# A four-layer graph network on one core: fixed ranges of 128 nodes in place of 52 pieces of the edge list with moving windows

## The chip, the cores and the metric

The kernel runs on one core of a Trainium2 chip. Times are device microseconds (us) of one execution. The profile is one more execution, recorded by the hardware profiler; its length is called the span. Lower is better.

## The reference

There are 6,250 nodes with 128 features and 206,250 directed edges, sorted by their destination; 6,250 of them go from a node to itself. Each edge has a source, a destination and 128 attributes of its own. Four layers follow one another, each with a residual and a layer norm:

```python
# layer 0: sums of the edge attributes by destination
agg = segment_sum(edge_attr, receivers); h = relu([agg, x] @ W1 + b1) @ W2 + b2
# layer 1: attention of 8 heads of 16; the softmax runs over ALL edges of a head
score = clip(sum(Q[dst] * K[src]) / 4, -5, 5); out[dst] += softmax(score) * V[src]
# then @ WO, layer norm, two-layer MLP, layer norm
# layer 2: an MLP for each edge, summed by destination, then an MLP for each node
e = relu([x[src], x[dst]] @ We1 + be1) @ We2 + be2; agg[dst] += e
# layer 3: graph convolution with degrees
agg[row] += x[col] / sqrt(deg[row] * deg[col]); out = agg @ W.T + b
```

The receivers of layer 0 are the sorted destinations. All data are float32, the indices int32.

## The kernel before

**Tiling.** Features lie on the 128 partitions and nodes on the columns, in an array of 6,656 columns (52 blocks of 128). The edge list is cut into NG = 52 pieces ("groups") of 31 x 128 = 3,968 rows; the last piece overlaps the one before. The destinations of a piece lie in a window of 128 nodes that starts at the piece's first destination. Where it starts is computed on the chip (`base`), and each use of a window first loads the value of `base` into a register (`window_start`, L153). Should a window not hold all destinations of a piece, a second pass would follow; the number of passes and rounds is found on the chip too (`passes0`, `rounds`), and is one for these inputs.

**Stage `prepare` (L217).** SP loads the indices and the weights. VectorE takes the minimum and maximum of each piece's destinations from an array `dst_i` with the pieces on 13 partitions (L263, L264), converts the indices, and makes for all edges at once the place in the window (`rel`), the block of 128 nodes in which the source lies (`bucket`), and the source's place in it (L269 to L288, `targets_of_pass` L194). Two of these arrays are also stored to DRAM (`sort_rel`, `sort_ids`, L232 to L235) for later.

**Stage `edge_sums_and_lists` (L441), layer 0's edges.** A loop over the 52 groups. SP loads 3,968 rows of attributes (L450). VectorE and ScalarE build a one-hot matrix of the destinations for each chunk of 128 rows (L565 for 19 chunks; L490 and L494 for 12), and TensorE multiplies it with the attributes, 24 chunks first (L638) and the other 7 later (L643). The result is added to the window (L586). In the same loop the edges of a group are sorted by the block of their source, for all later layers: a one-hot of the block (`bucket_hot`, L366), counts of each chunk (totals, L372), prefix sums over chunks and rows (L379, L383), the rank of each edge in its block (L390, L404), a one-hot of the rank (L408), and a product that puts the packed number of each edge in its slot (`pay` on POOL L415, codes L396), which is turned (L660) and stored as the group's list (L515). A list has 50 tiles of 128 slots: 49 blocks of sources and one tile for edges of a node to itself.

**Order.** TensorE's order in the loop is written out by hand: turn, sum of 24 chunks, totals of the next group, sum of the other 7, prefix of the next group, codes of this one. VectorE's is `rank_step` (chosen, reduce, the next bucket_hot, rank one-hot), target one-hot, add. Buffers are double.

**Edge layers 1 to 3.** `layer1_edges` (L1149) runs over 26 pairs of groups and in each group over the 50 tiles, in 13 batches of four. For each tile it builds a one-hot from the list on VectorE and ScalarE, gathers the rows of the sources with it on TensorE (L1360), gathers the queries of the window (L1363), and sums the messages by destination (L1375). `layer2_edges` (L1618) does the same for layer 2 (L1840, L1843, L1854, L1856; VectorE L1679 to L1703). It also counts the degrees and the edges to itself in two rows `counts`. `layer3_edges` (L2086) takes the blocks of sources by fours ("quads", 13 of them), and for each quad goes round all groups: counts (L2171), evacuation on ScalarE (L2147), spread (L2179), and after each quad an add of 512 columns (L2121). It first loads the window of each group from DRAM (`load_windows`, 52 transfers on two queues, L2081). At the end of each of these stages one group is prepared again for a further round (`resort_*`, L879 to L976), from `sort_rel` and `sort_ids`.

**Node stages.** `layer0_nodes` (L1020) takes 13 steps of two lanes of 256 nodes; the others take wide steps of four lanes and a rest of two. POOL splits the rows into bfloat16 parts (L815 to L826) for the gathers, and they are stored to DRAM. `layer2_nodes` (L1913) first turns the two rows of counts into columns with 104 matmuls of one column (L1918).

The lines in which a group's pieces and its windows come from:

```python
def load(j, b, at):
    sp.wait_ge(summed0, j + 1)
    sp.dma_start(edges[b][:, :, :], edge_attr[at, :].rearrange("(p c) f -> p c f", c=G)).then_inc(edges_in[b], 16)
```

Of the kernel before, what the change touches and what calls it, by code (L numbers as in the profile page):

```python
# [5 lines left out]
P = 128  # L6
D = 128
HEADS = 8
HEAD = D // HEADS
HIDDEN = 512  # L10
G = 31
SC = G * P
W = P
U = 1
T = 256
TJ = T // P
LANES = 2
LN_EPS = 1e-5
CLIP = 5.0

# [15 lines left out]
def sizes(n_nodes, n_edges):  # L36

    node_cols = -(-(n_nodes + W) // (LANES * T)) * LANES * T
    groups = -(-(-(-n_edges // SC)) // 4) * 4
    return node_cols, groups, groups  # L40


def gnn_program(nc, xT, edge_attr, src_index, src_id, dst_id, dst_rows, consts,
                w1, w2, wqkv, wo, aw1, aw2, we1, we2, wn1, wn2, w3t, vectors, row_bqkv, row_be1, row_be2, out):
    NODES = xT.shape[1]
    NG = src_id.shape[1] // G
    E = edge_attr.shape[0]
    NTILES = NODES // T
    STEPS = NTILES // LANES
    HI = NODES // P  # L50
    NB = HI - 3
# [4 lines left out]
    PAIRS = NG // 2  # L56
    SPR = NG // 4
    PASSES_MAX = NODES // W + 1
    ROUNDS_MAX = SC // P + 1
    assert SPR <= P and E >= SC and HI <= P and NG >= 4 and NODES < 2 ** 15 and BUCKETS <= 50  # L60
    ctx = ExitStack()
    with ctx:
# [26 lines left out]
        band = sb("band", [P, 2 * G - 1], BF16)  # L89
        before = sb("before", [G, G], BF16)  # L90
# [21 lines left out]
        base0 = sb("base0", [1, NG])  # L112
        n_passes = sb("n_passes", [1, 2])
# [15 lines left out]
        y_rows = dram("y_rows", (NODES, 3 * D), BF16)  # L129
        lists = dram("lists", (NG, 2, TILES * P), I16)  # L130
        sort_rel = dram("sort_rel", (P, NG, G))
        sort_ids = dram("sort_ids", (P, NG, 2, G), BF16)

# [7 lines left out]
        def passes0(eng):  # L141

            return eng.value_load(loops[0:1, 0:1], min_val=PAIRS, max_val=PAIRS * PASSES_MAX)

        def rounds(eng):

            return eng.value_load(loops[0:1, 1:2], min_val=PAIRS, max_val=PAIRS * PASSES_MAX * ROUNDS_MAX)
# [5 lines left out]
        def window_start(eng_type, g):  # L153

            return nc.values_load_multi_w_load_instructions(base[0:1, ds(g, 1)], engines=(eng_type,),
                                                            min_val=0, max_val=NODES - W)[1][0]
# [11 lines left out]
        rows_loaded = sem("rows_loaded")  # L168
        const_set = sem("const_set")
        dst_minmax = sem("dst_minmax")  # L170
        low_ready = sem("low_ready")
        range_max = sem("range_max")
        passes_set = sem("passes_set")
        split_ids = sem("split_ids")
        wq_scaled = sem("wq_scaled")
        biases_spread = sem("biases_spread")
        sort_stored = sem("sort_stored")
        moved0 = sem("moved0")
        prep_dma = 15
        MOVE = 4  # L180

        sort_scope = ExitStack()
        rel = sb("rel", [P, NG, G], scope=sort_scope)
        bucket0 = sb("bucket0", [P, NG, G], BF16, scope=sort_scope)
        lo1 = sb("lo1", [P, NG, G], BF16, scope=sort_scope)
        bucket = sb("bucket", [P, NG, G], BF16, scope=sort_scope)
        dr1 = sb("dr1", [P, NG, G], BF16, scope=sort_scope)
        inside = sb("inside", [P, NG, G], scope=sort_scope)
        rank_by4 = sb("rank_by4", [P, P, 4], BF16, scope=sort_scope)

        def flat(t):
            return t[:, :, :].rearrange("p s g -> p (s g)")

        def targets_of_pass(dve, done, by):  # L194

            dve.tensor_scalar(flat(inside), flat(rel), float(P), None, ALU.is_lt).then_inc(moved0, by)
            dve.wait_ge(moved0, done + by)
            dve.scalar_tensor_tensor(flat(inside), flat(rel), 0.0, flat(inside), ALU.is_ge, ALU.mult).then_inc(moved0, by)
            dve.wait_ge(moved0, done + 2 * by)
            dve.scalar_tensor_tensor(flat(bucket), flat(bucket0), 1.0, flat(inside), ALU.add,  # L200
                                     ALU.mult).then_inc(moved0, by)
            dve.tensor_scalar(flat(dr1), flat(rel), 1.0, None, ALU.add).then_inc(moved0, by)
            dve.wait_ge(moved0, done + MOVE * by)

        with ExitStack() as prep_scope:
            dst_i = sb("dst_i", [P, 4, SC], I32, scope=prep_scope)
            src_e = sb("src_e", [P, NG * G], I32, scope=prep_scope)
            dst_e = sb("dst_e", [P, NG * G], I32, scope=prep_scope)
            parts_e = flat(inside).bitcast(I32)
            src_f = sb("src_f", [P, NG * G], scope=prep_scope)  # L210
            same_e = sb("same_e", [P, NG * G], BF16, scope=prep_scope)[:, :]
            low_sb = sb("low_sb", [P, 8], scope=prep_scope)
            small = sb("small", [1, 4], scope=prep_scope)
            small_i = sb("small_i", [1, 4], I32, scope=prep_scope)
            bqkv_sb = sb("bqkv_sb", [1, 3 * D], scope=prep_scope)
            be1_sb = sb("be1_sb", [1, 2 * D], scope=prep_scope)
            with nc.Block("prepare") as block:  # L217
                @block.sync
                def _(sp):
                    sp.dma_start(dst_i[0:SPR, :, :], dst_rows).then_inc(rows_loaded, 16)  # L220
                    sp.dma_start(cst[:, :], consts).then_inc(rows_loaded, 16)
                    sp.dma_start(dst_e[:, :], dst_id).then_inc(rows_loaded, 16)
                    sp.dma_start(src_e[:, :], src_id).then_inc(rows_loaded, 16)
                    for tile, src in ((x, xT), (wqkv_sb, wqkv), (wo_sb, wo), (aw1_sb, aw1),
                                      (aw2_sb, aw2), (we2_sb, we2), (wn2_sb, wn2), (w3t_sb, w3t), (vec, vectors),
                                      (bqkv_sb, row_bqkv), (be1_sb, row_be1), (be2_sb, row_be2)):
                        sp.dma_start(tile[:, :], src).then_inc(loaded, 16)
                    sp.dma_start(we1_sb[:, 0:D], we1[0:D, :]).then_inc(loaded, 16)
                    sp.dma_start(we1_sb[:, D:2 * D], we1[D:2 * D, :]).then_inc(loaded, 16)
                    sp.dma_start(wn1_sb[:, :, :], wn1.rearrange("(b p) n -> p b n", p=P)).then_inc(loaded, 16)  # L230
                    sp.wait_ge(range_max, 4)
                    sp.dma_start(sort_rel, rel[:, :, :]).then_inc(sort_stored, 16)  # L232
                    sp.wait_ge(split_ids, 7)
                    sp.dma_start(sort_ids[:, :, 0, :], bucket0[:, :, :]).then_inc(sort_stored, 16)
                    sp.dma_start(sort_ids[:, :, 1, :], lo1[:, :, :]).then_inc(sort_stored, 16)  # L235
                    sp.wait_ge(sort_stored, 48)
                    sp.wait_ge(loaded, 16 * prep_dma)

                @block.vector
                def _(dve):  # L240
                    dve.memset(ones[:, :], 1.0).then_inc(const_set, 1)
# [170 lines left out]
        def pay_with(eng, pay, hot, vals):  # L412

            for w in range(2):
                last = eng.tensor_tensor(pay[:, :, w, :], hot[:, 0:G, :], over_columns(vals[w], BUCKETS), ALU.mult)  # L415
# [1969 lines left out]
```

## Time and profile before

| | before |
|---|---|
| median of 3 runs | 5670.74 us (5668.15 to 5678.23) |
| profiled execution | 5659.9 us span; a time of its own outside the span is not listed, the median of the runs is 10.8 us above it |
| TensorE busy | 5214.6 us (92%), 58,522 matmuls |
| VectorE busy | 4413.4 us (78%) |
| ScalarE busy | 3424.0 us (60%) |
| POOL busy | 2023.7 us (36%) |
| moved by DMA | 523.77 MB, mean 93 GB/s |

PE is TensorE's matmul, PEld its weight load, DVE VectorE, ACT ScalarE, SP the engine that issues most transfers. "SPq" and "ACTq" mark the issue of a transfer by that engine's queue. Busy time excludes waiting. The span falls into the start (to 117 us), layer 0's edges (to 777), its nodes (796 to 1019), layer 1's edges (1048 to 3053) and nodes (3086 to 3295), layer 2's edges (3327 to 4706) and nodes (4767 to 4886), layer 3's edges (4935 to 5533) and nodes (5565 to 5660).

### The profile page before, as it was taken

How to read it: one execution, taken by the hardware profiler on the slowest of the kernel's cores; microseconds unless marked ns; L12 is line 12 of the kernel's file. 1: busy time of each engine (PE TensorE's matmuls, PEld its weight loads, DVE VectorE, ACT ScalarE, POOL GpSimd, SP SyncE). 2: the span in 40 equal slices, each digit the busy share in tenths (PEclk: the TensorE clock that was granted, in tenths of full speed). 3: DMA queues.
4: the chain of work that ended last, by engine and by line, in shares of the span. 5: the costliest groups of instructions: out<-in, count | busy, mean ns of one | idle time of the engine just before them, and what ended most of it. 6: DMA issues, size and time to landing. Idle time of an engine off the chain costs nothing. (4 is left out here: it accounts for less than half of the span.)

```text
span 5659.9 us, 172717 instructions
## 1 busy us (share of the span) xinstructions
PE 5214.6 (92%) x58522; PEld 4657.6 (82%) x58522; DVE 4413.4 (78%) x7814; ACT 3424.0 (60%) x6098; POOL 2023.7 (36%) x1980
## 2 busy tenths in 40 slices
PE   2999989799999999999997879999999997699996
PEld 1888877699999999999997769999999996466655
DVE  6888852577777777777776669999999994488886
ACT  1445534577777777777774447777777772366651
POOL 1444436333333333333332545555555552300000
PEclk9999999899999999999998989999999997899998
DMA  6444421222222222222221133333333330200000
GB/s 108 158 164 169 162 81 67 95 96 93 89 95 95 87 95 95 89 94 95 91 91 39 50 104 129 134 130 134 131 134 128 136 129 19 67 1 0 0 0 25
DMA packets 206220, 523.77 MB, mean 93 GB/s; under 512 B 33555, under 2 KB 85398, under 8 KB 199318
## 3 DMA queue, kind: packets, MB, share of 16 engines
q1 hardware_dynamic: 195936, 518.35, 27.1%
q10 hardware_dynamic: 10179, 4.02, 0.3%
q8 instruction: 65, 1.06, 0.1%
q14 instruction: 40, 0.33, 0.0%
HBM read 485.12 MB, written 37.19 MB: 92 GB/s over the span
## 5 line engine op out<-in xcount | busy, mean ns | idle before, releaser
L1360 PE MATMUL ps<-kv_table,stage 128*128 128x256 bf16 x7644 | 1252.2, 273 | 29.9 <-ACT stage L1273 29.8
L1650 POOL TENSOR_TENSOR parts<-rest 128x512 bf16<-128x512 f32 x624 | 699.5, 1130 | 618.6 <-DVE rest L1703 618.5
L1840 PE MATMUL ps<-a_table,stage 128*128 128x128 bf16 x7644 | 842.6, 219 | 32.4 <-DVE stage L1679 32.4
L1843 PE MATMUL ps<-window,stage 128*128 128x128 bf16 x7800 | 861.1, 219 | 0.0
L1363 PE MATMUL ps<-window,stage 128*128 128x128 bf16 x7800 | 860.2, 219 | 0.0
L1331 POOL TENSOR_TENSOR message<-message 128x512 f32<-128x512 f32 (+1 forms) x468 | 472.7, 1010 | 948.8 <-ACT message L1280 948.8
L1196 DVE TENSOR_TENSOR product<-ps,q_kept 128x512 f32<-128x512 f32 (+1 forms) x676 | 452.3, 669 | 394.6 <-ACT message L1259 319.8
L1257 ACT ACTIVATE q_kept<-ps 128x512 f32<-128x512 f32 (+1 forms) x676 | 392.2, 580 | 576.9 <-PE ps L1363 568.0
L1360 PEld LDWEIGHTS ps<-kv_table,stage 128*128 128x128 bf16 x7644 | 669.4, 98 | 71.4 <-issue 30.4
L1363 PEld LDWEIGHTS ps<-window,stage 128*128 128x128 bf16 x7800 | 654.5, 98 | 59.3
L1759 ACT ACTIVATE parts<-ps 128x512 bf16<-128x512 f32 x624 | 370.2, 593 | 326.1 <-PE ps L1843 326.0
L1840 PEld LDWEIGHTS ps<-a_table,stage 128*128 128x128 bf16 x7644 | 534.7, 98 | 32.9 <-issue 32.9
L2179 PE MATMUL ps<-pairs,y_window 128*128 128x512 bf16 (+1 forms) x2028 | 532.8, 372 | 27.7 <-ACT pairs L2147 27.6
L1843 PEld LDWEIGHTS ps<-window,stage 128*128 128x128 bf16 x7800 | 545.5, 98 | 0.0
L2147 ACT ACTIVATE pairs<-ps 128x512 bf16<-128x512 f32 (+1 forms) x676 | 386.6, 572 | 260.1 <-PE ps L2171 211.4
L1375 PE MATMUL ps<-message,slot_hot 128*128 128x136 f32 x3536 | 514.3, 287 | 26.0 <-POOL message L1331 25.9
L1854 PE MATMUL ps<-parts,slot_hot 128*128 128x258 bf16 x2496 | 490.2, 273 | 2.1 <-DVE slot_hot L1695 1.6
L1856 PE MATMUL ps<-rest,slot_hot 128*128 128x128 bf16 x2600 | 475.9, 221 | 0.0
L1375 PEld LDWEIGHTS ps<-message,slot_hot 128*128 128x128 f32 x3536 | 442.1, 190 | 39.9 <-POOL message L1331 21.8
L1200 DVE TENSOR_REDUCE score<-product 128x32 f32<-128x512 f32 (+1 forms) x676 | 449.9, 666 | 23.9 <-DVE product L1196 0.9
L415 POOL TENSOR_TENSOR pay<-bucket_hot,vals 128x1550 bf16<-128x1550 bf16 x104 | 286.6, 2777 | 477.5 <-DVE rank_hot L408 368.8
L1208 DVE TENSOR_TENSOR slot_hot<-iota,slots 128x512 f32<-128x512 f32 (+1 forms) x676 | 452.9, 670 | 0.0
(359 smaller groups left out, 11002.7 us busy)
## 6 DMA issues: line engine op xcount, KB each, us to landing
stage<-lists SPq DMA_DIRECT2D x312, 768.0 KB, 4.1
edges<-in_edge_attr SPq DMA_DIRECT2D x52, 1984.0 KB, 7.6
stage<-lists SPq DMA_DIRECT2D x104, 896.0 KB, 5.4
window<-qkv_rows SPq DMA_DIRECT2D x52, 288.0 KB, 4.6
qkv_rows<-kv_table SPq DMA_DIRECT2D x26, 384.0 KB, 2.5
window<-ab_rows SPq DMA_DIRECT2D x52, 192.0 KB, 4.4
qkv_rows<-q_parts SPq DMA_DIRECT2D x26, 192.0 KB, 2.0
ab_rows<-a_table SPq DMA_DIRECT2D x26, 192.0 KB, 2.0
```

Of the source, the lines that this page charges most:

```text
L1196: dve.tensor_tensor(product[:, 0:nt, :], kv_ps[n % 2][:, 0:nt, 0:D], q_kept[n % 2][:, 0:nt, :], ALU.mult).then_inc(product1, 1)
L1208: dve.tensor_tensor(slot_hot[n % 2][:, 0:nt, :], over_chunks(iota1[:, :], nt), over_columns(slots[:, ds(g, 1), 0, 4 * b:4 * b + nt] .rearr ...
L1331: pool.tensor_tensor(values, values, message[n % 3][:, 0:nt, D:D + HEADS].unsqueeze(3) .broadcast_to([P, nt, HEADS, HEAD]), ALU.mult).then ...
L1360: nc.tensor.matmul(kv_ps[n % 2][:, i, :], from_src, kv_table[:, tile, q, :], start=(q == 0), stop=(q == 2))
L1363: last = nc.tensor.matmul(q_ps[n % 2][:, i, :], own, window[d][:, q * D:(q + 1) * D], start=(q == 0), stop=(q == 2))
L1375: last = nc.tensor.matmul(ps[:, 6 + d, 0:D + HEADS], slot_hot[n % 2][:, i, :], message[n % 3][:, i, :], start=(tile == 0), stop=(tile == S ...
L1650: pool.tensor_tensor(parts_of(n)[:, 0:nt, D:2 * D], rest[BUFFER[n]][:, 0:nt, :], middle[BUFFER[n]][:, 0:nt, :], ALU.subtract).then_inc(low ...
L1840: nc.tensor.matmul(to[:, i, :], from_src, a_table[:, tile, q, :], start=(q == 0), stop=False)
L1843: last = nc.tensor.matmul(to[:, i, :], own, window[d][:, (3 + q) * D:(4 + q) * D], start=False, stop=(q == 2))
L1854: nc.tensor.matmul(ps[:, 6 + d, 0:DIRECT], slot_hot[BUFFER[n]][:, :, i], parts_of(n)[:, i, :], start=(tile == 0), stop=False)
L1856: last = nc.tensor.matmul(ps[:, 6 + d, DIRECT:SUMS], slot_hot[BUFFER[n]][:, :, i], middle[BUFFER[n]][:, i, :], start=False, stop=(tile == ...
L2179: last = nc.tensor.matmul(ps[:, 4 + quad % 2, 0:nt * P], y_window[:, ds(i * 4 + d, 1), q * D:(q + 1) * D] .rearrange("p s f -> p (s f)"), ...
```

## The change

Groups are no longer pieces of equal length. There are NG = 49 fixed ranges of 128 nodes; group g has the nodes from 128 g on, and its part of the edge list is a piece of up to 35 chunks (SG = 4,480 rows) whose first row is found on the chip.

- The node arrays have 6,272 columns for 6,656. Windows need no `base`.
- In the start, the numbers of all edges (destination's block, place in the block, source's place, source's block; four bfloat16, 8 bytes a row) are computed in SBUF and stored to DRAM as `ids_rows`. The largest block in each run of 58 rows gives, by a comparison with all 49 groups and two reductions, the run in which each group begins (`best`, `low`, `begins`), and from it `base` (the piece's first row, at most E - SG) and `skip`. The minimum and maximum over `dst_i` go, and so do the stores `sort_rel` and `sort_ids`. `prepare` and `rounds` are no blocks of their own any more. Memsets of acc, slots, z_sum and deg are on POOL, the loads of x and of the sources on ScalarE's queue.
- In layer 0's loop, SP loads each group's numbers (4,480 rows of 8 bytes, 280 bytes a partition) two groups ahead. VectorE picks the rows that belong to the group (`id_step`, at the start of `rank_step`) before it builds bucket_hot; ScalarE's targets wait for it. ScalarE's copies `vals` (L484, L485) are gone, POOL reads the numbers. VectorE builds 20 chunks of targets, TensorE's first block has 27.
- The list's tile of edges of a node to itself takes those of the nodes whose place in their block is under 120.
- Node stages take 7 steps of 896 nodes (lanes of 256, 256, 256 and 128). Layer 0's are done by two lanes at a time, of 512 and 384 nodes.
- Edge layers run over 24 pairs and one single group. Layer 2's add has one more instruction for the edges to itself (`self_dis`), counts is one row, and `group_sum` has two buffers (TensorE's group matmuls wait for added2). The 104 matmuls of L1918 go.
- Layer 2's node steps put the parts of y in SBUF for layer 3 (`y_window`); the store `y_rows` and `load_windows` go.
- The group that is prepared again is loaded by one transfer of its numbers, and picked with 3 instructions for 5.

Counted from the reference's inputs, the largest range has 4,401 edges, or 4,408 with the rounding to runs of 58 rows; the largest list tile has 126 of 128 slots (124 for the edges to itself). So there is one pass and one round.

```diff
-G = 31
+G = 406
 SC = G * P
+RUN = 58
+RUNS = G // RUN
+GC = 35
+SG = GC * P
...
-    node_cols = -(-(n_nodes + W) // (LANES * T)) * LANES * T
-    groups = -(-(-(-n_edges // SC)) // 4) * 4
+    node_cols = -(-n_nodes // P) * P
+    chunks = -(-(-(-n_edges // SC)) // 4) * 4
...
+            def begins(dve, done, by):
+
+                dve.tensor_scalar(wanted[:, :], low[:, :], current[:, 0:1], None, ALU.add).then_inc(begun, by)
+                dve.wait_ge(begun, done + by)
+                dve.tensor_scalar(begin[:, :], wanted[:, :], float(E - SG), None, ALU.min).then_inc(begun, by)
+                dve.wait_ge(begun, done + 2 * by)
+                dve.tensor_copy(base[:, :], begin[0:1, :])
+                dve.tensor_tensor(skip[:, :], wanted[:, :], begin[:, :], ALU.subtract).then_inc(begun, by)
...
+                    sp.wait_ge(ids_stored, 48)
+
+                    sp.wait_ge(begun, 3)
+                    sp.wait_ge(passes_set, 1)
...
+                        def load_ids(g, b):
+                            at = first_edge(mybir.EngineType.SP, g)
+                            sp.dma_start(ids[:, ds(g, 1), :, :].rearrange("p s c w -> p (s c w)"),
+                                         ids_rows[ds(at, SG), :].rearrange("(p c) w -> p (c w)", c=GC)
+                                         ).then_inc(ids_in[b], 16)
+
+                        def load_edges(j, g, b):
+                            at = first_edge(mybir.EngineType.SP, g)
                             sp.wait_ge(summed0, j + 1)
                             sp.sem_inc(sp_waited, 1)
-                            sp.dma_start(edges[b][:, :, :], edge_attr[at, :].rearrange("(p c) f -> p c f", c=G)
+                            sp.dma_start(edges[b][:, :, :], edge_attr[ds(at, SG), :].rearrange("(p c) f -> p c f", c=GC)
                                          ).then_inc(edges_in[b], 16)
...
+                    dve.tensor_reduce(top[:, :], blocks_of(0, CH), AX.X, ALU.max).then_inc(edge_blocks, 1)
+                    dve.wait_ge(edge_blocks, 1)
+                    dve.wait_ge(const_set, 18 + CH)
+                    dve.tensor_tensor(reach, over_columns(iota[:, 0:NG], SUBS), over_chunks(top[:, :], NG), ALU.is_le
+                                      ).then_inc(edge_blocks, 1)
+                    dve.wait_ge(edge_blocks, 2)
+                    dve.tensor_tensor(keyed, reach, over_chunks(key_low[:, :], NG), ALU.mult).then_inc(edge_blocks, 1)
+                    dve.wait_ge(edge_blocks, 3)
+                    dve.tensor_reduce(best[0][:, :], keyed, AX.X, ALU.max).then_inc(edge_blocks, 1)
...
+                    def id_step(j, g, b, load):
+                        numbers = ids[:, ds(g, 1), :, :].rearrange("p s c w -> p (s c) w")
+                        dve.wait_ge(ids_in[b], load * 16 + 16)
+                        dve.wait_ge(hot_act0, j + 1)
+                        dve.tensor_scalar(owned[:, :], place[:, :], skip[:, ds(g, 1)], None, ALU.is_ge).then_inc(selected, 1)
+                        dve.wait_ge(selected, j * 2 + 1)
+                        inside_dve(dve, inside[:, :], owned[:, :], numbers[:, :, 0], g).then_inc(selected, 1)
+                        dve.wait_ge(selected, j * 2 + 2)
+                        dve.tensor_tensor(bucket[b][:, :], numbers[:, :, 3], inside[:, :], ALU.mult)
+                        dve.tensor_tensor(target[b][:, :], numbers[:, :, 1], inside[:, :], ALU.mult).then_inc(split_ids, 1)
...
+        LANES = ((0, T), (T, T), (2 * T, T), (3 * T, P))
...
-                        dve.tensor_tensor(counts[:, ds(at, P)], counts[:, ds(at, P)], GROUP_COUNTS, ALU.add)
...
+                        dve.tensor_tensor(self_dis[:, ds(g, 1)], self_dis[:, ds(g, 1)],
...
+        y_window = sb("y_window", [P, NG, 3, D], BF16)
...
-                    for c in range(HI):
-                        last = nc.tensor.matmul(ps[:, 7, c:c + 1], counts[:, c * P:(c + 1) * P], self_row[:, :],
-                                                start=True, stop=True)
...
-            def load_windows(eng, eng_type, odd):
```

## Rows read from the trace of the kernel before

**Rows 1.** Busy time by stretch: stretch, length, busy us (instructions) of each engine, granted clock, DMA.

```profile
core 0: us, PE busy (x) PEld busy (x) DVE busy (x) ACT busy (x) POOL busy (x), PEclk, DMA share, GB/s
...
777.00:796.00 19.00, 2.50 (x26) 1.67 (x23) 10.27 (x23) 2.31 (x5) 0.00 (x0) 0.64 0.14 44
796.00:1019.00 223.00, 216.64 (x988) 175.13 (x988) 56.16 (x130) 100.38 (x232) 134.29 (x194) 0.99 0.18 64
...
1048.00:3053.00 2005.00, 1963.39 (x20904) 1843.83 (x20904) 1563.48 (x3015) 1415.51 (x2495) 692.83 (x676) 1.00 0.26 92
...
3086.00:3295.00 209.00, 176.49 (x1040) 153.27 (x1040) 130.39 (x363) 90.90 (x297) 104.10 (x194) 0.96 0.14 45
...
3327.00:4706.00 1379.00, 1375.51 (x21216) 1355.60 (x21216) 1342.32 (x2079) 1007.69 (x1142) 732.21 (x676) 1.00 0.37 130
...
4767.00:4886.00 119.00, 116.10 (x572) 86.37 (x572) 50.27 (x152) 54.11 (x162) 51.25 (x97) 0.95 0.12 38
```

**Rows 2.** Timeline of one group of layer 0's loop: start us, us, engine, line, out<-in.

```profile
400.49 5.60 PE L638 MATMUL ps<-dst_hot,edges 128*128 128x128 f32 x48
...
406.02 0.97 PE L372 MATMUL ps<-bucket_hot,band 128*31 128x50 bf16 x31
...
406.92 1.83 PE L643 MATMUL ps<-dst_hot,edges 128*128 128x128 f32 x14
...
408.58 0.33 PE L379 MATMUL ps<-bucket_hot,lower 128*128 128x400 bf16 x1
...
408.88 0.29 DVE L586 TENSOR_TENSOR acc<-acc,ps 128x128 f32 x1 [0.27 <-PE ps L643]
...
410.82 1.60 PE L396 MATMUL ps<-pay,rank_hot 128*128 128x100 bf16 x31
...
413.12 5.60 PE L638 MATMUL ps<-dst_hot,edges 128*128 128x128 f32 x48
```

**Rows 3.** VectorE's groups in that loop: xcount | busy us, mean ns | idle before.

```profile
L565 DVE TENSOR_TENSOR dst_hot<-ps,rel 128x2432 f32<-128x2432 f32 x52 | 139.5, 2682 | 0.0
L408 DVE TENSOR_TENSOR rank_hot<-rank_by,rank_all 128x4096 bf16<-128x4096 bf16 x52 | 118.6, 2281 | 0.0
...
L390 DVE TENSOR_TENSOR chosen<-ps,bucket_hot 128x1600 f32<-128x1600 f32 x52 | 94.8, 1824 | 97.1 <-PE ps L383 97.1
L404 DVE TENSOR_REDUCE rank_all<-chosen 128x1600 f32 (+1 forms) x52 | 94.6, 1820 | 7.8 <-DVE chosen L390 7.8
```

**Rows 4.** Timeline of the start, 0 to 118 us.

```profile
2.38 5.61 DVE L245 MEMSET acc<- 128x6656 f32 x1 [1.38 <-issue]
...
16.56 0.15 DVE L253 TENSOR_SCALAR lane<-cst 128x1 f32<-128x1 f32 x1 [5.47 <-DMA src_e<-in_src_id]
...
34.36 16.66 DVE L264 TENSOR_REDUCE low_sb<-dst_i 13x4 f32<-13x15872 int32 x1
...
56.75 1.84 DVE L276 SCALAR_TENSOR_TENSOR lo<-bucket,src_f 128x1612 bf16<-128x1612 bf16 x1
...
107.09 1.77 DVE L366 TENSOR_TENSOR bucket_hot<-ps,bucket 128x1550 bf16<-128x1550 f32 x1 [0.38 <-DVE list_b L554]
...
117.28 6.96 PE L638 MATMUL ps<-dst_hot,edges 128*128 128x128 f32 x48
```

**Rows 5.** Timeline of the start of layer 3's edges.

```profile
4903.47 1.29 PE L2171 MATMUL ps<-src_hot,dst_hot 128*128 128x128 bf16 x8 [18.13 <-DVE src_hot L2113]
...
4934.00 1.57 ACT L2147 ACTIVATE pairs<-ps 128x512 bf16<-128x512 f32 x3 [48.71 <-issue]
```

**Rows 6.** The add after each quad of layer 3: duration min/median/max, first and last start.

```profile
L2121 DVE TENSOR_TENSOR acc<-acc,ps x11: 686/686/689, 5029.1 to 5489.3; 128x512 f32<-128x512 f32 x11
```

**Rows 7.** DMA issues: count, KB each, median us from issue to landing.

```profile
sort_rel<-rel SPq DMA_DIRECT2D x1, 806.0 KB, 3.7
...
sort_ids<-lo SPq DMA_DIRECT2D x1, 403.0 KB, 35.6
...
stage<-sort_ids SPq DMA_DIRECT2D x2, 15.5 KB, 1.7
```

**Rows 8.** Timeline ahead of layer 2's node steps.

```profile
4741.29 22.34 PE L1918 MATMUL ps<-self_row,counts 2*128 2x1 f32 x104 [3.47 <-DVE self_row L1977]
```

More of the change, by code:

```diff
@@ new lines, in node_tiles, with norm_pe @@
+            tiles["inv"] = [sb(f"inv{layer}_{l}", [P, T // P], scope=scope) for l in range(lanes)]
+            return tiles
+        ALL = range(ROUND)
+        def norm_pe(pe, t, nth, ready, before_ready, lanes=ALL, bank=half, buffer=lambda l: l):
+            for k, l in enumerate(lanes):
+                b = buffer(l)
+                pe.wait_ge(ready, before_ready + k + 1)
+                nc.tensor.matmul(bank(b, 1)[:, 0:width(l)], centre_m, t["res"][b][:, 0:width(l)], start=True, stop=True
+                                 ).then_inc(centred_ps, 1)
+            for k, l in enumerate(lanes):
+                b = buffer(l)
+                pe.wait_ge(squared, nth + k + 1)
+                for j in range(blocks(l)):
+                    last = nc.tensor.matmul(bank(b, 2)[:, j:j + 1], t["sqr"][b][:, j * P:(j + 1) * P], mean_col[:, :],
@@ L1488, in _ @@
+                        norm_act(act, t, nth1(n, 2))
+                        for l in ALL:
+                            act.wait_ge(normed, nth1(n, 2) + l + 1)
+                            act.activation(x[:, columns(n, l)], t["y"][l][:, 0:width(l)], ACT.Copy).then_inc(x_kept, 1)
+                    with loop(act, 0, STEPS) as n:
+                        step(n)
                 @block.vector
@@ L1566, in _ @@
+                    with loop(sp, 0, STEPS) as n:
+                        step(n)
+                    for l in ALL:
+                        sp.wait_ge(ab_stored[l], STEPS * 32 + 32)
                         sp.sem_inc(sp_waited, 1)
@@ new lines, in add, with body @@
+                        dve.tensor_tensor(counts[:, ds(g * P, P)], counts[:, ds(g * P, P)], GROUP_COUNTS, ALU.add)
+                        dve.tensor_tensor(acc[:, ds(g * P, P)], acc[:, ds(g * P, P)], GROUP_ACC, ALU.add).then_inc(added2, 1)
+                    def body(j, g, behind, groups=2):
+                        for n in range(groups * BATCHES):
+                            d, b = n // BATCHES, n % BATCHES
+                            if n + 1 < groups * BATCHES:
+                                rest_of(j + (n + 1) // BATCHES, n + 1)
+                            elif groups == 2:
+                                rest_of(j + 2, 0)
+                            slots_of(j + d, g + d, n)
@@ L1966, in step @@
+                        for l in ALL:
                             act.wait_ge(normed, nth2 + first + l + 1)
[L1967 to L1969 removed]
+                            act.activation(x[:, columns(n, l)], t["y"][l][:, 0:width(l)], ACT.Copy).then_inc(x_kept, 1)
+                    with loop(act, 0, STEPS) as n:
+                        step(n)
                 @block.vector
@@ L2222, in _ @@
+                            four(first, quad, 0, begin=True)
+                            with loop(pe, 1, FOURS - 1) as i:
+                                four(first, quad, i)
                             four(first, quad, FOURS - 1, end=True)
+                            if quad + 1 < QUADS:
+                                count(first, quad + 1, 1, 1)
+                            spread(first, quad, NG - 1, 0, end=True)
                         resort_pe(pe, again, step3, first, again_total)
```

2143 lines of the change are left out of this document (1113 added, 1030 removed).

## The prediction

> **What bounds the kernel now.** I read the busy times by stretch first, since the mean share of TensorE over the span says nothing of one stage. In the three long edge stretches TensorE is busy for 1963 of 2005 us, 1375.5 of 1379 us and, in the node steps between, 217 of 223 us, at a granted clock of 0.99 to 1.00, which is the upper level, 2.4 GHz [rows 1]. VectorE follows it closely only in layer 2 (1342 of 1379). So what counts is how many matmuls the program has, and the edge stages have a fixed number for each group. Then I read one group of the first loop in order of time [rows 2] and VectorE's groups of the same loop [rows 3]; there the reader is to see that TensorE goes from one matmul block to the next without a gap, and that VectorE's only long idle time is the wait for the prefix sums (97 us in 52 groups). Last come the stretches in which TensorE has nothing to do: the first 117 us, the seams between layers and the 29 us ahead of layer 3's first spread [rows 4, 5].
>
> **The edge layers, groups of a fixed cost.** A group keeps 50 tiles of 128 slots whatever its number of edges; 49 groups for 52 take three away. Layer 1: 2005 / 52 = 38.56 us each [rows 1], times 3 is -116. With 24 pairs and one single group the last one has no partner to overlap; I bound that at 16 us (under half a group): -116 to -100. Layer 2: 1379 / 52 = 26.52, times 3 is -80. It gains a VectorE instruction of 128x1 for each group; the nearest row is a 128x1 at 0.15 us [rows 4], 49 of them 7 us on an engine with 37 us to spare in that stretch: nothing, and +15 if its hand-off shows. The sums' second buffer makes TensorE wait for added2 where ScalarE waited before; queued behind that wait are the next tile's matmuls, but the add that it waits for is a group (26 us) old. Layer 3: one quad goes round all groups in 46.02 us, (5489.3 - 5029.1) / 10 [rows 6]; 46.02 x 3 / 52 = 2.65 less, for 12 full quads and a shorter 13th at about 2.5: -34.
>
> **Layer 0's loop, fewer groups of more chunks.** Here the edges are the same, and a piece grows from 31 to 35 chunks, so this goes up. The period now is 413.12 - 400.49 = 12.63 us [rows 2]: sums 5.53 + 1.66, totals 0.90, prefix 2.24, codes 1.60 and 0.70 up to the next sum. Chunks scale by 35/31, the prefix by 9/8 (nine chunks to a bank for eight): 8.12 + 1.02 + 2.52 + 1.81 + 0.70 = 14.17. Times 49 is 694, against 12.63 x 52 = 657: +38. VectorE's work for a group by the same scaling [rows 3]: chosen 2.05, reduce 2.05, buckets 1.99, ranks 2.57 (36 columns of chunks for 32), targets 2.82 (20 chunks for 19), add 0.29 [rows 2], and four id instructions of 35 columns, by the 128x1 at 0.15 about 0.75 with two hand-offs: 12.5 us. (Buckets from the 1.77 in [rows 4].) It stays 1.6 under TensorE's 14.17. The id step stands between the reduce and the bucket instruction, and delays the latter; from the prefix's end that is 2.05 + 2.05 + 0.75 + 1.99 = 6.8 us, and the totals that need it come 1.81 + 0.70 + 6.3 = 8.8 us after it. 2 us are over, so the added wait is hidden. ScalarE's target instructions now wait for the same step (split_ids); they start some 3 us later and have the whole sum block as cover. Bounds: +30 if the sums are a little better packed, +103 if VectorE becomes the bound at 15.5 us a group.
>
> **The ids' loads.** Each group gets a 35 KB load from DRAM in 280-byte pieces, two groups ahead of its use, on SP's queue between the loads of the edges. The nearest row is a 15.5 KB load of the same fields at 1.7 us [rows 7]. Twice that is 3.5 us in a period of 14.17: cost nothing in the loop, 3.5 once at the start. SP's edge loads are queued behind the wait for the ids before; as these landed a group earlier, nothing waits. A row that bears against it is the removed store: 62-byte pieces took 35.6 us for 403 KB, long pieces 3.7 us for 806 KB [rows 7]. The Trainium skill ("DMA: Bandwidth & Descriptors", Specifications) says that a transfer under 512 bytes loses the full rate because the DMA engine then reads, modifies and writes. By that page the loads would be slow and the sum 2 to 5 us higher at the start, no more while two groups of cover stand. The 15.5 KB load in 62-byte pieces, at 1.7 us, shows no such loss on the reading side, and the sum goes by it.
>
> **The start.** The first sum now begins at 117.28 [rows 4]. Two reductions over all targets on 13 partitions (16.7 us each, one behind the other) go, and so does the slow store with the barrier behind it: the last long field instruction of before starts at 56.75, the loop's first at 107.09. In their place the ids arrive at about 10 (four loads had landed by 16.56, and now the targets come first, the sources on ScalarE's queue); 8 field instructions at 1.84 are 14.7; 8 searches over 49 x 28 runs at about 1.5 (by size from the 1.84) are 12; some 25 small dependent instructions at 0.3 are 7.5; constants and conversions 5; together the first rows are known near 50. The long-piece store runs beside the searches. One id load and the loop's own 10.2 us from the bucket instruction to the first sum, 12 with 35 chunks, lead to 66: -51. Bounds: -62 if searches and fields overlap, -35 if each hand-off takes double. What is queued behind SP's new waits there (ids stored, first rows found, constants moved) is the first edge load, needed at about 66: on the path only if those waits end much after 55. The memsets of acc (5.61 us on VectorE [rows 4]) go to POOL, which has nothing else until 50: nothing lost, at most 6 us either way; with the x load moved to the other queue I put -2.
>
> **Seams and node steps.** The seam after layer 0's loop is 19 us, 10.3 of them VectorE's [rows 1]: the targets of a second pass are no longer made, and the limits come without a barrier of their own: -5 (-9 to 0). Layer 0's nodes: 13 steps took 223 us for 6656 columns; 6272 are 0.942 of that, -13 by columns, one step more gives back 2: -11 (+17 if POOL's splitting, 134 us busy, ends up behind the narrower steps). Layer 1's nodes: 209 us, -12 by columns, +11 for one more wide step and POOL's last splits: -1 (-12 to +8). Layer 2's, 119 us, -7 and +2: -5. Layer 3's, which move as many columns in as many steps, I scale from layer 2's: -4. The three places that redo a group for the lists now load the ids by one DMA and do 3 instructions for 5, but first wait for a value read on SP: +2 each, +6 (0 to +10).
>
> **Layer 2 to 3.** 104 matmuls of one column at the low clock, 22.34 us with all else waiting [rows 8], go with counts' second row: -23 with their hand-off. Layer 3 loaded its windows from DRAM in 52 transfers: the count ends at 4904.8 and the first evacuation starts at 4934.00 [rows 5]. Filled in SBUF by the node steps, it is there at once, and what is late next is the count itself: -29 (-20 if POOL's last splits are late).
>
> **Sum.** -116 - 80 - 34 + 38 - 51 - 2 - 5 - 11 - 1 - 5 - 4 + 6 - 23 - 29 = -317 us. The profiled span is 5659.9, so the span after is 5343; the median of the three times is 10.8 above the span, which gives **5354 us**.
>
> **Rivals.**
> A, layer 0's loop bound by VectorE. For it: 12.5 of 14.17 leaves little, and in [rows 3] its ends are dependent. Against: the 97 us of idle that are there now. At 15.5 us a group, 65 more: 5419.
> B, the id step exposed in each group: load landing and step stand ahead of the totals, 3.5 us x 49 = 172: 5526. Against: two groups of cover.
> C, slower: a group's rows don't fit its piece. The piece has 4480 rows and its start is only found to 58 rows; from 4480 on a second pass is made, of the loop (694) and, as each pass and round repeats it, of the edge stages (1889 + 1300 + 564) and of the redoing of 49 groups at each: some 17,700 us. By counting the inputs the largest range has 4401 edges, and 4408 with the rounding, so it should not come; only a mistake of the search on the chip would bring it.
> D, the fixed ranges bring nothing: the edge stages are bound by tiles in use, not by groups. Against it stand 52 equal group times; then the 230 us of the edge layers stay, and only the other terms hold: 5584.
>
> **How the numbers follow.** Forecast 0.82, A 0.09, B 0.03, D 0.02, C 0.03, and 0.01 for gains that meet losses within 0.2%, 11 us, which is about what a measurement of this kernel can tell. The forecast's own bounds added in part (start +16, single group +16, nodes +25; start -11, loop -8, seam and nodes -6) give 5329 to 5411; with A the range is 5315 to 5425, a little wider at both ends for what no row shows. Faster: 0.96, same 0.01, slower 0.03.
>
> **What would show it.** The first sum near 66 us. 14.2 us from sum to sum in layer 0, VectorE still idle ahead of chosen (about 1.5 us a group; none under A). Layer 1's edge stretch near 1889, layer 2's near 1300, quads at 43.4. No one-column matmuls ahead of layer 2's node steps, and the first evacuation of layer 3 within 2 us of the count. It would be wrong by A if the loop is 15.5, by a start later than 85, or by a node stage longer than before.

## The result, and the profile after

The changed kernel takes 5488.94 us (median of 4 runs, 5486.88 to 5493.09) against 5671.44 us for the kernel before (4 runs, 5668.15 to 5678.23): a ratio of 0.9678, interval 0.9665 to 0.9692. It is faster by 182 us where 317 were forecast, and lies outside the range of 5315 to 5425. The profiled span is 5485.0 us, 174.9 less than before. It lies 3.9 us under the median of the runs, where the forecast added 10.8: the forecast misses the span by 142 us and the time by 135, and these 7 us are luck.

Busy time by stretch of the changed kernel (columns as in [rows 1]):

```profile
0.00:70.00 70.00, 11.12 (x87) 6.67 (x87) 50.27 (x69) 18.70 (x28) 16.47 (x16) 1.00 0.44 167
70.00:824.00 754.00, 662.89 (x8664) 589.75 (x8662) 728.39 (x479) 350.46 (x956) 297.59 (x96) 1.00 0.40 148
...
838.00:1086.00 248.00, 209.50 (x1023) 168.87 (x1024) 60.22 (x135) 96.93 (x247) 141.76 (x224) 0.93 0.19 66
1086.00:2977.00 1891.00, 1850.12 (x19696) 1737.05 (x19696) 1471.60 (x2839) 1334.11 (x2350) 653.12 (x637) 1.00 0.26 92
2977.00:3263.00 286.00, 189.51 (x1142) 165.01 (x1143) 158.09 (x433) 97.43 (x329) 111.02 (x224) 0.82 0.13 40
3263.00:4586.00 1323.00, 1304.23 (x19983) 1278.92 (x19982) 1294.69 (x2004) 949.00 (x1076) 684.66 (x637) 1.00 0.36 128
4586.00:4767.00 181.00, 129.32 (x699) 98.40 (x699) 79.10 (x201) 54.21 (x179) 54.06 (x112) 0.77 0.00 1
4770.00:5356.00 586.00, 569.14 (x4224) 344.94 (x4297) 477.91 (x1277) 363.19 (x635) 0.00 (x0) 0.96 0.00 0
5356.00:5485.00 129.00, 85.41 (x615) 70.59 (x614) 79.26 (x250) 21.71 (x94) 0.00 (x0) 0.87 0.08 26
```

The second line is the one to stop at: in layer 0's loop VectorE is busy for 728 of 754 us and TensorE only for 663. Before, TensorE set the pace there. Against the forecast, by the marks in both traces (first sum, first gather, last group matmul of a layer, first count):

| stretch | before | after | difference | forecast |
|---|---|---|---|---|
| to the first sum | 117.3 | 70.0 | -47 | -53 |
| layer 0's loop and the seam | 678.5 | 767.8 | +89 | +33 |
| layer 0's nodes, to layer 1's first gather | 252.7 | 248.2 | -4.5 | -11 |
| layer 1's edges | 2005 | 1891 | -114 | -116 |
| one group again, layer 1's nodes | 274 | 285.5 | +11 | +1 |
| layer 2's edges | 1378.4 | 1324.5 | -54 | -80 |
| one group again, layer 2's nodes, to the first count | 198 | 180 | -18 | -26 |
| first count to first spread | 31.2 | 2.2 | -29 | -29 |
| layer 3's quads | 598.4 | 586.7 | -12 | -34 |
| one group again, layer 3's nodes | 126.9 | 128.6 | +2 | -2 |

Of the 142 us by which the span misses the forecast, the loop has 56, layer 2's edges 26, the quads 22, the start 6, and the node stages with what lies around them some 30.

One group of layer 0's loop after the change (answers to [rows 2]; start us, us, engine, line):

```profile
406.28 6.22 POOL L278 TENSOR_TENSOR pay<-bucket_hot,ids 128x1750 bf16<-128x1750 bf16 x2 [9.43 <-DVE rank_hot L271]
...
408.69 0.77 DVE L661 TENSOR_SCALAR owned<-place,skip 128x35 bf16<-128x35 f32 x1
408.75 1.65 PEld L260 LDWEIGHTS ps<-pay,rank_hot 128*128 128x128 bf16 x35
...
409.64 2.91 DVE L283 SCALAR_TENSOR_TENSOR inside<-ids,cst,owned 128x35 bf16<-128x35 bf16 x1 [0.19 <-DVE owned L661]
...
412.69 0.20 DVE L665 TENSOR_TENSOR bucket<-ids,inside 128x35 bf16<-128x35 bf16 x1
...
412.94 2.03 DVE L254 TENSOR_TENSOR chosen<-ps,bucket_hot 128x1800 f32<-128x1800 f32 x1
...
419.07 1.07 PE L236 MATMUL ps<-bucket_hot,band 128*35 128x50 bf16 x35 [1.52 <-DVE bucket_hot L230]
...
424.39 1.78 PE L260 MATMUL ps<-pay,rank_hot 128*128 128x100 bf16 x35
```

The period is 424.39 - 408.75 = 15.64 us here; over all groups it is 15.45 on average. POOL's pay is two instructions, 6.22 us in all, so the first ends near 409.4 and the second at 412.50. VectorE's owned, of 35 columns, ends at 409.46, and inside, of 35 columns too, at 412.55: each ends just after one of POOL's ends. That is no chance of this group: in each of the 48 groups whose step stands in the loop, inside ends between 0.05 and 0.06 us behind pay. And chosen, which could start once the prefix is done at 408.8, starts at 412.94; TensorE then waits 1.52 us for bucket_hot, ahead of the totals. The same two instructions while POOL is idle, in the start of the same trace:

```profile
33.51 0.40 SPq L372 DMA_DIRECT2D ids_rows<-dst_hot  x1
...
56.74 1.56 SPq L392 DMA_DIRECT2D ids<-ids_rows  x2
58.69 0.24 DVE L661 TENSOR_SCALAR owned<-place,skip 128x35 bf16<-128x35 f32 x1 [3.90 <-DMA ids<-ids_rows]
58.97 0.26 DVE L283 SCALAR_TENSOR_TENSOR inside<-ids,cst,owned 128x35 bf16<-128x35 bf16 x1
...
70.03 1.22 PE L798 MATMUL ps<-dst_hot,edges 128*128 128x128 f32 x4
```

0.24 and 0.26 us, against 0.77 and 2.91; POOL starts its first pay only at 62.04. The add (acc<-acc,ps) starts beside pay in each group too and keeps its 0.28 us; it reads one of its two operands from PSUM. Layer 2's added instruction shows the same pattern (timeline, then the same line's durations, min/median/max):

```profile
4003.69 1.05 POOL L1864 TENSOR_TENSOR parts<-rest 128x512 bf16<-128x512 f32 x1 [1.26 <-DVE rest L1923]
4003.77 0.99 DVE L1929 TENSOR_TENSOR self_dis<-self_dis,group_sum 128x1 f32 x1
...
L1929 DVE TENSOR_TENSOR self_dis<-self_dis,group_sum x49: 158/992/996, 3306.8 to 4587.4; 128x1 f32 x46, 128x1 f32<-128x1 f32 x3
```

It starts 0.08 us behind POOL's instruction and ends 0.02 us behind its end.

### The profile page after: what moved, and what is told of

Its sections match the earlier page's. It is cut to its first block and busy times, and to the rows that moved or that the text cites. A ratio compares the mean times of both kernels' runs of the same rounds, so it can differ in the third digit from the quotient of the medians.

```text
span 5485.0 us, 164969 instructions
## 1 busy us (share of the span) xinstructions
PE 5016.6 (91%) x56178; PEld 4464.3 (81%) x56254; DVE 4408.0 (80%) x7721; ACT 3289.6 (60%) x5897; POOL 1958.7 (36%) x1946
## 5 line engine op out<-in xcount | busy, mean ns | idle before, releaser
L1555 PE MATMUL ps<-kv_table,stage 128*128 128x256 bf16 x7203 | 1180.0, 273 | 29.7 <-ACT stage L1461 29.5
L1864 POOL TENSOR_TENSOR parts<-rest 128x512 bf16<-128x512 f32 x588 | 654.0, 1118 | 613.3 <-DVE rest L1923 607.0
L2062 PE MATMUL ps<-a_table,stage 128*128 128x128 bf16 x7203 | 794.6, 219 | 41.2 <-DVE stage L1899 41.2
L2065 PE MATMUL ps<-window,stage 128*128 128x128 bf16 x7350 | 812.1, 219 | 0.0
L1558 PE MATMUL ps<-window,stage 128*128 128x128 bf16 x7350 | 810.8, 219 | 0.0
L1555 PEld LDWEIGHTS ps<-kv_table,stage 128*128 128x128 bf16 x7203 | 629.5, 98 | 69.2 <-issue 30.3
L1558 PEld LDWEIGHTS ps<-window,stage 128*128 128x128 bf16 x7350 | 616.9, 98 | 55.9
L2062 PEld LDWEIGHTS ps<-a_table,stage 128*128 128x128 bf16 x7203 | 504.2, 98 | 41.8 <-issue 41.6
L2065 PEld LDWEIGHTS ps<-window,stage 128*128 128x128 bf16 x7350 | 514.5, 98 | 0.0
L1570 PE MATMUL ps<-message,slot_hot 128*128 128x136 f32 x3332 | 484.7, 287 | 24.3 <-POOL message L1519 24.3
L2372 PE MATMUL ps<-pairs,y_window 128*128 128x512 bf16 (+1 forms) x1835 | 490.9, 372 | 3.7 <-ACT pairs L2341 0.2
L278 POOL TENSOR_TENSOR pay<-bucket_hot,ids 128x1750 bf16<-128x1750 bf16 x98 | 303.8, 3121 | 502.7 <-DVE rank_hot L271 451.5
```

Source lines behind the costliest of these rows:

```text
L1555: nc.tensor.matmul(kv_ps[n % 2][:, i, :], from_src, kv_table[:, tile, q, :], start=(q == 0), stop=(q == 2))
L1558: last = nc.tensor.matmul(q_ps[n % 2][:, i, :], own, window[d][:, q * D:(q + 1) * D], start=(q == 0), stop=(q == 2))
L1570: last = nc.tensor.matmul(ps[:, 6 + d, 0:D + HEADS], slot_hot[n % 2][:, i, :], message[n % 3][:, i, :], start=(tile == 0), stop=(tile == S ...
L1864: pool.tensor_tensor(parts_of(n)[:, 0:nt, D:2 * D], rest[BUFFER[n]][:, 0:nt, :], middle[BUFFER[n]][:, 0:nt, :], ALU.subtract).then_inc(low ...
L2062: nc.tensor.matmul(to[:, i, :], from_src, a_table[:, tile, q, :], start=(q == 0), stop=False)
L2065: last = nc.tensor.matmul(to[:, i, :], own, window[d][:, (3 + q) * D:(4 + q) * D], start=False, stop=(q == 2))
```

## The experiments

Theory 1: a VectorE instruction with two operands in SBUF, or one with a single operand in a fast form, is held until POOL's running instruction ends; the step that the change adds was put where POOL is busy, in layer 0 and in layer 2. The rivals: VectorE simply has too much work (2), the ids arrive late (3), anything on VectorE beside pay is slow (4), layer 2 loses to its other new wait or to the single last group (5). The gains below compare medians with the changed kernel's 5488.94 us. The kernel before, measured along with each series, gave 5671, 5668 and 5666 us, so such a difference is good to some 5 us; the profiled spans fall by 52 us in e1, 73 in e2, 17 in e3 and 22 in e4.

**e1, the id step behind the reduce.**

```diff
-                        if load is not None:
-                            id_step(j + 1, g + 1, 1 - b, load)
                         dve.wait_ge(prefixed, j + 2)
...
                         if load is not None:
+                            id_step(j + 1, g + 1, 1 - b, load)
                             bucket_step(j + 1, 1 - b)
```

> The four id instructions stand behind the rank reduce in place of ahead of chosen; nothing else moves. Theory 1 (a VectorE instruction that reads two SBUF operands, or a single one in its fast form, is held until POOL's running pay instruction ends): at the new place pay is over, so the inside instruction takes about 0.26 us for 2.90, a group's period falls from 15.64 to 14.2 to 14.5 us, and the kernel from 5489 to about 5425 us. Rival 2 (VectorE has too much work in a group, wherever the step stands): inside stays near 2.9 us and the period at 15.6. Rival 3 (the ids' loads arrive late): the period stays and the wait for the load shows ahead of owned.

5432.67 us, ratio to before 0.9585 (0.9569 to 0.9601): 56 us off the changed kernel. VectorE's groups in the loop (answers to [rows 3]):

```profile
L254 DVE TENSOR_TENSOR chosen<-ps,bucket_hot 128x1800 f32<-128x1800 f32 x47 | 95.5, 2033 | 82.0 <-PE ps L247 82.0
...
L283 DVE SCALAR_TENSOR_TENSOR inside<-ids,cst,owned 128x35 bf16<-128x35 bf16 x46 | 11.8, 257 | 8.6 <-DVE owned L661 8.6
L661 DVE TENSOR_SCALAR owned<-place,skip 128x35 bf16<-128x35 f32 x46 | 10.8, 235 | 0.0
```

The same instructions are short at the other place, and the idle time ahead of chosen is back (82 us). Rival 2 falls. So does rival 3: there is no wait for a load ahead of owned here, and in the changed kernel only one, for the first group. From the codes of the first group to those of the last the period is 14.33 us.

**e2, the id step at its early place, its results in PSUM.**

```diff
-            owned = sb("owned", [P, GC], BF16, scope=scope)
-            inside = sb("inside", [P, GC], BF16, scope=scope)
+            owned = ps[:, 2, 256:256 + GC]
+            inside = ps[:, 2, 320:320 + GC]
...
```

> The id step stays at its early place, while pay runs, but owned and inside are written to PSUM, so that inside, bucket and target read one operand from SBUF and one from PSUM. Theory 1 in its narrow form (what is held is the second SBUF read): inside takes under 0.4 us with pay running, the period falls to 14.3 to 14.7 us, the kernel to about 5430 us. Rival 4 (any VectorE instruction of this kind that runs beside pay is slow): inside stays near 2.9 us and nothing changes. The owned instruction has one SBUF operand and a PSUM output now; if only it stays at 0.7 us, that was its wait for the first half of pay.

5415.29 us, ratio 0.9558 (0.9542 to 0.9573): 74 us off, 17 more than e1. Timeline of one group:

```profile
400.94 6.21 POOL L278 TENSOR_TENSOR pay<-bucket_hot,ids 128x1750 bf16<-128x1750 bf16 x2 [7.94 <-DVE rank_hot L271]
...
404.00 0.26 DVE L661 TENSOR_SCALAR ps<-place,skip 128x35 f32<-128x35 f32 x1
404.45 0.26 DVE L283 SCALAR_TENSOR_TENSOR ps<-ids,cst,ps 128x35 f32<-128x35 f32 x1 [0.19 <-DVE ps L661]
404.85 0.19 DVE L665 TENSOR_TENSOR bucket<-ids,ps 128x35 bf16<-128x35 f32 x1
...
405.98 2.03 DVE L254 TENSOR_TENSOR chosen<-ps,bucket_hot 128x1800 f32<-128x1800 f32 x1 [0.81 <-PE ps L247]
```

POOL's pay runs from 400.94 to 407.15, all three stand inside it, and none is held. So it is not POOL's running as such (rival 4 falls), but where the operands lie. Bucket and target still write to SBUF, have one operand in PSUM now, and take 0.19 us each beside pay: a write to SBUF alone is not held. Owned has the same inputs as before and only its output has moved; whether it was held for a fast form or for something else about that output no run tells apart. Chosen waits for TensorE again, and the period is 14.0 us, (754.8 - 82.8) / 48 from the first group's codes to the last's: a little under the 14.17 of the sum. The Trainium skill ("SBUF — State Buffer", Who interferes with whom) has the rule: VectorE and GpSimd (POOL) share one pair of SBUF ports as an exclusive lock, and whichever comes first keeps it for its whole instruction. A VectorE instruction with two SBUF inputs contends with a GpSimd instruction that reads SBUF, one in a 2-port mode with any; one with at most one SBUF input and outside these modes does not contend. The trace agrees: inside takes 2.91 us with both inputs in SBUF and 0.26 us with one in PSUM.

**e3, layer 2's add reads PSUM.**

```diff
                         dve.tensor_tensor(self_dis[:, ds(g, 1)], self_dis[:, ds(g, 1)],
-                                          group_sum[d][:, 2 * D + 1:DIRECT], ALU.add)
+                                          ps[:, 6 + d, 2 * D + 1:DIRECT], ALU.add)
...
                         if b == 0:
                             pe.wait_ge(group_sb2, j + 1)
+                            pe.wait_ge(added2, j + ready - 1)
```

> Layer 2 only: the added 128x1 instruction reads the group's sum from PSUM in place of SBUF, and TensorE's first scatter of a group waits for the add of two groups before. Theory 1: self_dis falls from 0.98 us to under 0.3, some 34 us of VectorE's time; the edge stretch of layer 2 goes from 1323 to about 1300 us, the kernel by as much. Rival 5 (the 26 us of layer 2 come from TensorE's wait for added2 or from the single last group): self_dis gets short, the stretch stays at 1323.

5468.2 us, ratio 0.9646 (0.963 to 0.9663): 21 us off. The line's durations:

```profile
L1929 DVE TENSOR_TENSOR self_dis<-self_dis,ps x49: 139/142/157, 3305.7 to 4567.7; 128x1 f32 x46, 128x1 f32<-128x1 f32 x3
```

0.142 us for 0.992, and layer 2's edges take 1306 us for 1324.5. Here only an input has moved to PSUM, and the output stays in SBUF. The kernel has one wait more on TensorE and is still faster, so rival 5 falls for 18 of the 26 us; the last few (1306 against some 1299 forecast) stay open.

**e4, layer 3 in turns of eight groups.** The quads took 45.1 us where 46.02 x 49 / 52 = 43.4 was forecast. Theory 6: the difference is what TensorE pays for each turn of its inner loop. Rival 7: it is the phase between the engines at the border of a quad.

```diff
-                            with loop(pe, 1, FOURS - 1) as i:
+                            with loop(pe, 1, FOURS - 1, 2) as i:
                                 four(first, quad, i)
+                                four(first, quad, i + 1)
```

> Layer 3 only: TensorE's inner loop takes eight groups a turn for four. Theory 6 (the 1.7 us that a quad takes over 49 x 0.882 us are TensorE's turns of the loop, some 0.13 us each with no instruction ready): half the turns, quads at about 44.4 for 45.1 us, some 8 us less in all. Rival 7 (it is the phase between the engines at the border of a quad): quads stay at 45.1 us.

5465.92 us, ratio 0.9644 (0.9627 to 0.966): 23 us off, three times what was expected. The adds after each quad (answer to [rows 6]), first of the changed kernel, then of e4:

```profile
L2315 DVE TENSOR_TENSOR acc<-acc,ps x13: 286/687/689, 4814.8 to 5356.1; 128x512 f32<-128x512 f32 x12, 128x128 f32<-128x128 f32 x1
```

```profile
L2315 DVE TENSOR_TENSOR acc<-acc,ps x13: 289/687/689, 4814.8 to 5333.9; 128x512 f32<-128x512 f32 x12, 128x128 f32<-128x128 f32 x1
```

Divided by 12 these are 45.1 and 43.3 us a quad. What the turn costs can be seen at TensorE's weight loads once in four groups, in the changed kernel:

```profile
5012.44 0.27 PEld L2364 LDWEIGHTS ps<-src_hot,dst_hot 128*128 128x128 bf16 x4 [0.43 <-issue]
...
5016.22 0.26 PEld L2364 LDWEIGHTS ps<-src_hot,dst_hot 128*128 128x128 bf16 x4 [0.49 <-issue]
```

and in the kernel before, in turns of four as well:

```profile
5131.96 0.27 PEld L2171 LDWEIGHTS ps<-src_hot,dst_hot 128*128 128x128 bf16 x4 [0.30 <-issue]
...
5135.45 0.32 PEld L2171 LDWEIGHTS ps<-src_hot,dst_hot 128*128 128x128 bf16 x4 [0.25 <-issue]
```

Before, the gap stays within the lead that weight loads have over the matmuls: around these two places the counts start evenly, 0.88 or 0.89 us apart. After, it is 0.13 to 0.24 us longer and the next matmul starts late, 1.01 and 1.07 us behind the count before it. In e4's trace, with eight groups a turn, the counts from 4945 to 4961 us are even again, through two turns. Rival 7 falls, and theory 6 holds in that longer turns take the loss away; my size, half of the loss, was too small. It is not the turn alone, since the kernel before had turns of four without a loss.

**e6, the same turns of four, code moved.** Theory 8: it matters where the loop's code lies.

```diff
+                    for _ in range(32):
+                        pe.sem_inc(pe_waited, 1)
                     with pe.Fori(0, total, NG) as first:
```

> Layer 3's turns of four groups as in the changed kernel, but with 32 more one-word instructions on TensorE's queue ahead of the loop, which shift where its code lies and cost about 1 us themselves. Theory 8 (what makes the turn cost is where the loop's code falls): the layer's stretch changes clearly, by 5 us or more from 586. Theory 6 in its plain form (a turn of four groups costs this wherever it lies): within 2 us of 586.

The adds of the quads:

```profile
L2315 DVE TENSOR_TENSOR acc<-acc,ps x13: 289/687/689, 4819.1 to 5360.2; 128x512 f32<-128x512 f32 x12, 128x128 f32<-128x128 f32 x1
```

(5360.2 - 4819.1) / 12 = 45.1 us, unchanged (5490.94 us, one run). This one shift of the code does not move it; other shifts were not tried. Why the turn is longer after the change than before, with the same number of matmuls in it, stays open.

**e5, all three.** The edits of e2, e3 and e4 together.

> The id step's two results in PSUM, layer 2's add from PSUM, and layer 3's turns of eight groups, together. The three places lie in stages that follow one another, so the gains should add: 74 + 21 + 23 = 118 us off 5489, which is 5371 us, 17 above the blind forecast. If one gain had only moved a wait that another stage gives back, the sum comes out smaller: over 5380 us.

5380.16 us (5375.16 to 5384.15), ratio to before 0.9497 (0.9484 to 0.951), the fastest of all. The median lies 9 us over the 5371 expected, just at the 5380 above which the expectation said that the gains do not add. But the 118 us were a sum of differences of medians from different series. By stage they add: the span is 5373.3, 112 less than the changed kernel's, and 73 + 17 + 22 = 112 are the three spans' gains one by one. The loop with its seam gives 70 of them, layer 2 takes 1303 us for 1324.5, and a quad 43.3. The time is 26 us over the blind forecast and the span 30, as much as the node stages and what lies around them missed, which none of the three edits touches.

## Why the prediction was wrong

**The mechanism was right for the groups.** Layer 1's three groups were worth 114 us for 116. The wait for windows went as forecast (-29), the stretch around the one-column matmuls gave 18 of 26, and the start brought 47 of 53. There the first rows were known at 43.4 us, before the 50 forecast, but the number of passes only at 54, a last link that my chain of searches did not have.

**The step that failed** is "four id instructions of 35 columns, by the 128x1 at 0.15 about 0.75 with two hand-offs: 12.5 us", then "It stays 1.6 under TensorE's 14.17", and with it "the added wait is hidden". By size the price was nearly right: they are 0.9 us of work in e1 and e2, 1.2 with the hand-offs. But I placed the step between the reduce and the bucket instruction; the code has it at the start of `rank_step`, ahead of chosen, as my own list of the changes says. There POOL's pay is running, and chosen started 412.94 - 408.69 = 4.25 us after the step did. With it VectorE's round is 15.5 to 15.6 us in most groups, not 12.5, and it sets the pace. I took the price of a small instruction from a row in which POOL is idle (0.15 us [rows 4]) and used it for a place where POOL is at work. Rival A had the right outcome for the loop (15.5 us a group, +65; measured 15.45 on average, and 56 over the forecast with the seam) with a chance of 0.09, but not the cause: it rested on 12.5 of 14.17 leaving little, and by work alone there was room enough (e2). Even where I had placed the step it would not have been hidden: e1 has it there and takes 14.42 us in most groups, for the 14.17 of the sum.

**The same mistake in layer 2**: "49 of them 7 us on an engine with 37 us to spare in that stretch: nothing". They took 46.8 us of VectorE's time at 0.98 each; of the 26 us missed e3 gave back 18 to 21. The kernel before could have told it, in the stage from which those 37 us were read. Its line L1679, with one tensor operand, in SBUF, ahead of the stage with POOL idle and in the stage beside POOL:

```profile
3326.46 0.61 DVE L1679 TENSOR_SCALAR stage<-stage,lane 128x1536 bf16<-128x1536 int16 x1
...
3336.82 1.06 POOL L1650 TENSOR_TENSOR parts<-rest 128x512 bf16<-128x512 f32 x1 [1.79 <-DVE rest L1703]
3336.89 1.40 DVE L1679 TENSOR_SCALAR stage<-stage,lane 128x1536 bf16<-128x1536 int16 x1
```

The same instruction takes 0.61 and 1.40 us. The latter starts behind POOL's and ends 0.41 us behind its end, and so do all 206 of that stage that start beside POOL, within 0.41 to 0.49 us. This is read from the trace; no run moved it. So some 160 us of VectorE's 1342 busy us there were waiting already, an estimate from 206 x (1.40 - 0.61).

**The quads**: the term "46.02 x 3 / 52 = 2.65 less" took the cost of a group as it was, and the changed loop pays more for each turn of four. e4 shows 43.3 us with longer turns, e6 that one shift of the code does not matter; why the turn costs more is open.

**The node stages** (some 30 us) I scaled by columns. In layer 1's, the steps and the tail behind them tell. TensorE's last matmul, POOL's last split and the next layer's first matmul, in the changed kernel:

```profile
3218.28 3.19 PE L1666 MATMUL ps<-early,y 128*128 128x256 f32 x14
...
3240.03 0.43 POOL L974 TENSOR_TENSOR b_parts<-ab_rest,b_parts 128x128 bf16<-128x128 f32 x1 [0.18 <-POOL b_parts L971]
...
3262.70 0.50 PE L2062 MATMUL ps<-a_table,stage 128*128 128x128 bf16 x3 [41.23 <-DVE stage L1899]
```

and in the kernel before:

```profile
3291.33 3.51 PE L1466 MATMUL ps<-early,y 128*128 128x256 f32 x8
...
3303.85 0.67 POOL L826 TENSOR_TENSOR b_parts<-ab_rest,b_parts 128x256 bf16<-128x256 f32 x1 [0.18 <-POOL b_parts L823]
...
3327.23 0.50 PE L1840 MATMUL ps<-a_table,stage 128*128 128x128 bf16 x3 [32.39 <-DVE stage L1679]
```

The last step had two lanes before and has four after, so POOL's splits run 19.0 us past TensorE's end for 9.7, and the idle time ahead of the next layer grows from 32.4 to 41.2 us, by 9. That tail the forecast had, in its +11 for one more wide step and POOL's last splits. What did not come is the -12 by columns: the steps themselves took 210 us for 211, seven full steps for six and a short one. TensorE's granted clock in them was 0.91 for 0.95, which may be a part of it. This is read from the traces, no run tested it.

**What did not happen**: the ids' loads never held the loop (rival B), though they land later there than forecast:

```profile
ids<-ids_rows SPq DMA_DIRECT2D x49, 35.0 KB, 7.1
...
stage<-ids_rows SPq DMA_DIRECT2D x2, 35.0 KB, 1.8
```

7.1 us behind the edges' transfer, 1.8 us alone, for the same 35 KB in 280-byte pieces. Against the 1.7 us of the 15.5 KB load in 62-byte pieces [rows 7], and 1.9 us for a load of 96 KB in pieces of 768 bytes in the kernel before (y_window<-y_rows), transfers of this size show no loss for short pieces on the reading side. The rule weighed in the forecast (the Trainium skill, "DMA: Bandwidth & Descriptors", Specifications) is not seen here on loads; larger loads in short pieces were not measured. There was no second pass (rival C; the rows give 694 + 1889 + 1300 + 564 us for one, and I can't derive its 17,700 us from them), and the stretches fell with the number of groups (rival D falls): layer 1 took 1891 / 49 = 38.6 us a group, as before.

## What to carry to other kernels

Price a small instruction with the row of the place where it will stand. If POOL is running beside it and it reads two operands from SBUF, its price is what is left of POOL's instruction: 2.9 us here for 0.26 us of work, and 0.99 us for the 0.14 us of a single column. Look for the same line with POOL idle and with POOL at work in the trace that you have. Two cures were seen: keep one operand in PSUM (74 us), or move the step to where the other engine is idle (56 us). Apart from that, in a loop whose pace is set by TensorE, make each turn longer where the turn shows ahead of a weight load (23 us).

## What the runs showed of the hardware that I had not expected

A held VectorE instruction counts as busy for the whole time that it waits. The profile gave inside as 2.9 us of work and VectorE as 97% busy; only the ends, within 0.1 us of POOL's, told that it was waiting. And in e1, where nothing is held, the step's later place still costs 17 us against e2. ScalarE's targets wait for it, 2.6 us a group in that trace, and behind them on the same engine stands the copy of the totals that TensorE's prefix needs. The prefix's row in e1 (85 to 750 us):

```profile
L243 PE MATMUL ps<-bucket_hot,lower 128*128 128x450 bf16 x184 | 66.9, 364 | 9.5 <-ACT totals L492 9.5
```

In e1 the prefix waits for the totals in 48 of 49 groups, 0.2 us each behind the first, and its weight load 0.4 us; in e2 it waits for them once, in the start. That fits the 14.42 us against 14.04 of most groups; no run moved it alone.
